# Attention and a mixture of experts in one kernel: a stack of its own for row-tiled scores, padded stacks for full-array distances, and a new order of down projection and scores

## What is computed

```python
B, S, D = 32, 256, 128            # x is (32, 256, 128); 16 heads of 8
x = x + attention(layernorm(x))   # attn = stablemax3(q k^T / sqrt(8)), out = attn v, then w_out and b_out
x = x + experts(layernorm(x))     # 4 experts of 512, the 2 best of each token by softmax of the router
# experts: h = silu(x w1[e]) * (x w3[e]); out = sum over e of gate[e] * (h w2[e])
# stablemax3(l): l -= max(l); s = 1/(1 - l(1 - l/2 (1 - l/3))) for l < 0; s / sum(s)
```

## Time and profile before

| | |
|---|---|
| three runs | 1270.7, 1271.81, 1272.38 us; median 1271.81 us |
| profiled execution | 1271.22 us, of which the span of the instructions is 1269.5 us |
| busy share | PE 89%, PEld 72%, DVE 78%, ACT 79%, POOL 57% |
| DMA | 77.58 MB, 19.7% of 16 DMA engines on the main queue |
| costliest groups | POOL L391 399.2 us; ACT L515 259.3 us; the three groups of PE L874 324.4, 293.4 and 292.9 us; DVE L651 308.5 us |
| mean granted TensorE clock | 0.980 |

### The profile page before, as it was taken

How to read it: one execution, slowest core, us unless ns; L and a number is a source line. 1 busy time by engine, 2 the same in 40 slices (tenths; PEclk the granted TensorE clock), 3 DMA queues, 4 the chain that set the end, 5 groups by cost and what they waited for, 6 DMA issues and landing times.

```text
span 1269.5 us, 29119 instructions
## 1 busy us (share of the span) xinstructions
PE 1135.1 (89%) x10116; PEld 911.3 (72%) x10116; DVE 985.9 (78%) x1804; ACT 1006.8 (79%) x1033; POOL 724.0 (57%) x961
## 2 busy tenths in 40 slices
PE   2569999899999999999999999999999999999987
PEld 1347777677877777777777787777777777778777
DVE  5678888788888887888888888888788887788632
ACT  1788888888888888888788888788888788888852
POOL 2426655565665556665556566555666555656554
PEclk9969999999999999999999999999999999999999
DMA  5112222102222211222211222221122221122000
GB/s 164 54 52 69 70 74 74 54 30 67 72 68 72 70 44 40 67 68 72 72 53 29 67 72 68 72 66 44 44 67 68 72 72 52 32 64 70 27 22 26
DMA packets 85034, 77.58 MB, mean 61 GB/s; under 512 B 11136, under 2 KB 79360, under 8 KB 84992
## 3 DMA queue, kind: packets, MB, share of 16 engines
q1 hardware_dynamic: 84560, 76.64, 19.7%
q10 hardware_dynamic: 432, 0.39, 0.1%
HBM read 53.81 MB, written 21.10 MB: 59 GB/s over the span
## 4 chain that ended last, share of the span: by engine, by line
PE 64%; DVE 15%; issue 12%; ACT 4%; DMA 2%; POOL 1%; DVEq 1%; SPq 0%; POOLq 0%; ACTq 0%
PE banks L874 21%; PE banks L1064 20%; PE sc L931 5%; PE banks L892 5%; DVE mx L727 4%; DVE hid L643 4%; PE sc L1049 3%; ACT w_sq L515 3%; DVE poly L651 2%; PE misc L1112 2%; PE misc L1015 2%; PE misc L1113 1%; PE misc L996 1%; POOL hid L391 1%; PE banks L1049 1%
## 5 line engine op out<-in xcount | busy, mean ns | idle before, releaser
L391 POOL TENSOR_TENSOR hid<-hid,gate_all 128x512 f32<-128x512 f32 x256 | 399.2, 1595 | 201.9 <-DMA gate_all<-gate_scratch 168.5
L515 ACT ACTIVATE w_sq<-sc 128x1024 f32<-128x1024 f32 x256 | 259.3, 1026 | 157.4 <-PE sc L931 157.1
L874 PE MATMUL banks<-xn_hi,w_hi 128*128 128x256 f32 x1024 | 324.4, 317 | 64.0 <-issue 28.5
L651 DVE SCALAR_TENSOR_TENSOR poly<-w_sq,sc 128x1024 f32<-128x1024 f32 x256 | 308.5, 1216 | 58.2 <-ACT w_sq L515 53.0
L874 PE MATMUL banks<-xn_lo,w_hi 128*128 128x256 f32 x1024 | 293.4, 287 | 0.0
L874 PE MATMUL banks<-xn_hi,w_lo 128*128 128x256 f32 x1024 | 292.9, 286 | 0.0
L874 PEld LDWEIGHTS banks<-xn_hi,w_hi 128*128 128x128 f32 x1024 | 197.6, 193 | 117.9 <-issue 75.9
L1064 PE MATMUL banks<-w_sb,hid 128*128 128x128 f32 x2048 | 268.0, 283 | 13.6 <-DVE hid L643 10.7
L1064 PEld LDWEIGHTS banks<-w_sb,hid 128*128 128x128 f32 x2048 | 240.0, 191 | 37.4 <-DVE hid L643 17.4
L727 DVE TENSOR_REDUCE mx<-sc 128x4 f32<-128x1024 f32 x192 | 228.5, 1220 | 42.2 <-PE sc L1049 40.4
L574 ACT ACTIVATE poly<-poly,two 128x2048 f32<-128x2048 f32 x128 | 254.9, 1992 | 0.4
(11 more groups left out here) (96 smaller groups left out, 1211.5 us busy)
## 6 DMA issues: line engine op xcount, KB each, us to landing
qk_scratch<-qk_split SPq DMA_DIRECT2D x32, 512.0 KB, 3.1
gate_all<-gate_scratch SPq DMA_DIRECT2D x32, 512.0 KB, 4.4
k_stack<-qk_scratch SPq DMA_DIRECT2D x96, 128.0 KB
q_stack<-qk_scratch SPq DMA_DIRECT2D x93, 128.0 KB
x_in<-in_L_attn_x_dram SPq DMA_DIRECT2D x32, 128.0 KB, 2.1
x_res<-in_L_attn_x_dram SPq DMA_DIRECT2D x32, 128.0 KB, 2.3
out_dram<-y_acc SPq DMA_DIRECT2D x32, 128.0 KB, 1.8
hid<-in_L_ffn_w_dram SPq DMA_DIRECT2D x2, 1024.0 KB, 6.5
```

The lines of the kernel that those rows point to most:

```text
L391: nc.gpsimd.tensor_tensor(h, h, by_token.unsqueeze(1).to_broadcast([128, 2, C, 128]), ALU.mult).then_inc(gated, 1)
L515: nc.scalar.activation(w_sq[:, u % 2, :], sc[:, u % 2, :], ACT.Square).then_inc(sq_ok, 1)
L651: nc.vector.scalar_tensor_tensor(poly[:, u, :], w_sq[:, u % 2, :], 3.0, sc[:, u % 2, :], ALU.add, ALU.mult).then_inc(poly_ok, 1)
L874: last = nc.tensor.matmul(dst, lhs[a], rhs[b], start=(k == 0), stop=(k == len(terms) - 1))
```

## The change

Scores and distances no longer share a stack.

- **Tiles for the scores.** q_tile and k_tile, one buffer each, hold the layout of 32 partitions a head, now with four terms (lo lo is added) and no row of maxima. Eight transfers fill them each step, of 128 KB. They wait until the scores of the sequence before are through (s_full).
- **Padded stacks for the distances.** q_stack has 8 groups of two heads, 64 partitions a head, row 8d + r; rows 124 to 127 take the maxima. k_pad holds for each head j of a pair its own 64 partitions and zeros elsewhere, which are written once at the start, as are the ones that meet the maxima. So a distance contracts over all 128 partitions and takes its head alone. Four transfers of 128 KB fill q_stack, eight of 64 KB fill k_pad. The matmuls' number and their 256 columns stay: 4 for a unit. Only units above 1 wait for poly_ok; unit 0 waits for the stacks and the maxima.
- **Order.** On TensorE score 0 stands ahead of the down projection, three of its units between score 0 and score 1, down(1,3) behind the transposes, maxima_T ahead of up_a of unit 0, and in the first half up_a of unit 6 ahead of the output projection. On VectorE maxima_out stands ahead of experts_added.
- **Wait.** up_a_unit(0) no longer waits for acc_ok.

```diff
-    STEP = 4
-    MROW, MSTEP = 3, 16
+    TERMS = 4
+    HALF = 64
+    MROW = 124
+    STEP = HALF // HD
+    GP = H // 2
...
-        q_stack = [sb(f"q_stack{i}", [128, G, S], F32R) for i in range(2)]
-        k_stack = [sb(f"k_stack{i}", [128, G, S], F32R) for i in range(2)]
-        no_maxima = sb("no_maxima", [8, S])
+        q_tile = sb("q_tile", [128, G, S], F32R)
+        k_tile = sb("k_tile", [128, G, S], F32R)
+        q_stack = [sb(f"q_stack{i}", [128, GP, S], F32R) for i in range(2)]
+        k_pad = [sb(f"k_pad{i}", [128, GP, 2, S], F32R) for i in range(2)]
+        ones = sb("ones", [2, S])
...
-        STACKED = 16 * 7
+        TILED = 16 * 2 * TERMS
+        STACKED = 16 * 12
...
-            eng.memset(k_stack[par][:].bitcast(F32), 1.0).then_inc(blank[par], 1)
+            eng.memset(k_pad[par][:].bitcast(F32), 0.0).then_inc(blank[par], 1)
...
+        def tile_rows(tile, r):
+            return tile[r::TERMS, :, :].bitcast(F32)
+
+        def tile_part(part):
+            return scratch[part].rearrange("(g e) t -> e g t", g=G)
...
         def stack_rows(stack, r):
             return stack[r::STEP, :, :].bitcast(F32)
 
         def stack_part(part):
-            return scratch[part].rearrange("(g e) t -> e g t", g=G)
+            return scratch[part].rearrange("(g e) t -> e g t", g=GP)
+
+        def pad_rows(pad, r, j):
+            return pad[HALF * j + r:HALF * (j + 1):STEP, :, j, :].bitcast(F32)
+
+        def pad_part(part, j):
+            return scratch[part].rearrange("(g j d) t -> j d g t", g=GP, j=2)[j]
...
+                    after(sp, tiled, tiles_read)
...
                 if has(i, off + 1):
+                    sp.wait_ge(qk_stored, stored_qk)
+                    after(sp, s_full, scored)
+                    for r, part in enumerate((1, 3, 1, 3)):
+                        sp.dma_start(tile_rows(k_tile, r), tile_part(part)).then_inc(tiled, 16)
+                    for r, part in enumerate((0, 0, 2, 2)):
+                        if isinstance(i, int) and n == -1:
+                            continue
+                        sp.dma_start(tile_rows(q_tile, r), tile_part(part)).then_inc(tiled, 16)
                     after(sp, w_full, w_used)
-                    sp.wait_ge(qk_stored, stored_qk)
                     if isinstance(i, int) and 0 <= n + 1 < 2:
                         sp.wait_ge(blank[par], 2)
-                    for r, part in enumerate((1, 3, 1)):
-                        sp.dma_start(stack_rows(k_stack[par], r), stack_part(part)).then_inc(stacked[par], 16)
-                    sp.dma_start(q_stack[par][MROW::MSTEP, :, :].bitcast(F32),
-                                 no_maxima[:].unsqueeze(1).to_broadcast([8, G, S])).then_inc(stacked[par], 16)
-                    for r, part in enumerate((0, 0, 2)):
+                        for j in range(2):
+                            sp.dma_start(k_pad[par][MROW + 2 * j:MROW + 2 * j + 2, :, j, :].bitcast(F32),
+                                         ones[:].unsqueeze(1).to_broadcast([2, GP, S])).then_inc(ones_in[par], 16)
+                    for r, part in enumerate((0, 0, 2, 2)):
                         if isinstance(i, int) and n == -1:
                             continue
                         sp.dma_start(stack_rows(q_stack[par], r), stack_part(part)).then_inc(stacked[par], 16)
+                    for r, part in enumerate((1, 3, 1, 3)):
+                        for j in range(2):
+                            sp.dma_start(pad_rows(k_pad[par], r, j), pad_part(part, j)).then_inc(stacked[par], 16)
...
-                    sp.dma_start(q_stack[par][MROW::MSTEP, :, :].bitcast(F32), m_split[:]).then_inc(m_stacked[par], 16)
+                    sp.dma_start(q_stack[par][MROW:, :, :].bitcast(F32), m_split[:]).then_inc(m_stacked[par], 16)
...
                 m = no(i, off)
                 after(pe, silu_ok, UP * m + u)
                 if u == 0:
-                    after(pe, acc_ok, m)
                     pe.wait_ge(xn2_lo_ok, m + 1)
                 up(u, up_a, w1_hi, w1_lo, a_full)
 
...
-            def distance_of(i, off, g, h, c):
-                par, rows = off % 2, slice(TILE * h, TILE * (h + 1))
-                at = (C * (h % 2) + c) * S
-                return nc.tensor.matmul(sc[:, h // 2, at:at + S], k_stack[par][rows, g, c * 128:(c + 1) * 128],
-                                        q_stack[par][rows, g, :], start=True, stop=True)
-
-            def first_distances(i, off):
+            def distances(i, off, u):
+
                 m, par = no(i, off), off % 2
-                pe.wait_ge(s_used, U * (m + 1))
-                pe.wait_ge(m_stacked[par], pair_count(i, off, 16))
-                for c in range(C):
-                    for h in range(4):
-                        op = distance_of(i, off, 0, h, c)
-                        if c == C - 1 and h % 2:
-                            op.then_inc(w_full, 1)
-
-            def distances(i, off, u):
-
-                m = no(i, off)
-                pe.wait_ge(poly_ok, U * m + u - 1)
-                for c in range(C):
-                    for h in (2 * (u % 2), 2 * (u % 2) + 1):
-                        last = distance_of(i, off, u // 2, h, c)
+                if u == 0:
+                    pe.wait_ge(s_used, U * (m + 1))
+                    pe.wait_ge(stacked[par], pair_count(i, off, STACKED))
+                    pe.wait_ge(m_stacked[par], pair_count(i, off, 16))
+                    if isinstance(i, int) and 0 <= m < 2:
+                        pe.wait_ge(ones_in[par], 32)
+                elif u > 1:
+                    pe.wait_ge(poly_ok, U * m + u - 1)
+                for j in range(2):
+                    for c in range(C):
+                        at = (C * j + c) * S
+                        last = nc.tensor.matmul(sc[:, u % 2, at:at + S], k_pad[par][:, u, j, c * 128:(c + 1) * 128],
+                                                q_stack[par][:, u, :], start=True, stop=True)
                 last.then_inc(w_full, 1)
...
-                if has(i, off):
-                    first_distances(i, off)
+                distance(0)
+                distance(1)
...
                 distance(6)
+                if has(i, off - 2):
+                    up_a_unit(i, off - 2, 6)
...
                     last.then_inc(res_full, 1)
-                if has(i, off - 2):
-                    up_a_unit(i, off - 2, 6)
                 distance(7)
...
                     if g == 0:
                         after(pe, poly_ok, U * m)
-                        pe.wait_ge(stacked[par], pair_count(i, off + 1, STACKED))
+                        pe.wait_ge(tiled, TILED * (m + 1))
...
-                                                  q_stack[par][rows, g, c * 128:(c + 1) * 128],
-                                                  k_stack[par][rows, g, :], start=True, stop=True)
+                                                  q_tile[rows, g, c * 128:(c + 1) * 128],
+                                                  k_tile[rows, g, :], start=True, stop=True)
...
                 down(0, 0)
                 down(0, 1)
-                score(0)
                 down(0, 2)
+                score(1)
                 down(0, 3)
```

More of the change, by code:

```diff
@@ L179, in attention_then_experts_kernel @@
         m_ok = sem("m_ok")
+        ones_in = [sem(f"ones_in{i}") for i in range(2)]
+        tiled = sem("tiled")
         m_stacked = [sem(f"m_stacked{i}") for i in range(2)]
@@ L527, in first_half @@
                     act.wait_ge(qk_stored, 16)
+                    for r, part in enumerate((0, 0, 2, 2)):
+                        nc.scalar.dma_start(tile_rows(q_tile, r), tile_part(part)).then_inc(tiled, 16)
                     act.wait_ge(blank[0], 2)
-                    for r, part in enumerate((0, 0, 2)):
+                    for r, part in enumerate((0, 0, 2, 2)):
                         nc.scalar.dma_start(stack_rows(q_stack[0], r), stack_part(part)).then_inc(stacked[0], 16)
@@ L840, in second_half @@
                     shifted_logits()
+                if has(i, off + 1):
+                    maxima_out()
                 if has(i, off - 2):
                     experts_added()
-                if has(i, off + 1):
-                    maxima_out()
                 if has(i, off + 2):
@@ L1114, in queries_and_keys @@
                                      stop=True).then_inc(qk_full, 1)
+                score(0)
                 down(0, 0)
                 down(0, 1)
-                score(0)
                 down(0, 2)
+                score(1)
                 down(0, 3)
-                score(1)
                 down(1, 0)
+                score(2)
                 down(1, 1)
-                score(2)
                 down(1, 2)
-                down(1, 3)
                 score(3)
@@ L1131, in second_half @@
                     queries_operand()
+                down(1, 3)
                 if isinstance(i, int) and n == 0:
@@ L1139, in second_half @@
```

(4 more changed lines are left out.)

21 lines of the change are left out of this document (11 added, 10 removed).

## The result

The changed kernel takes 1184.53 us (median of 4 runs, 1183.5 to 1186.13) against 1272.1 us, a ratio of 0.9314 (95% interval 0.9298 to 0.933). The forecast was 1199 us: right in sign and range, 14.5 us too slow.

The account below looks back on a forecast made before the run. No engine is full; TensorE's waits once per sequence, chiefly 1.60 us before the first up, were taken as the bound. 1271.2 - 67.3 (29 x (0.71 + 1.61)) - 8.3 clock + 3.5 start = 1199 us, range 1178 to 1228.

Parts of the forecast that it names:

- the clock: Lower-clock spells behind TensorE's long hole at up_a of unit 0 go with it: 8.3 us in 29 sequences.
- the start: First sequence: ten more transfers before the expert weights, 6.4 us, 2.95 hidden in ScalarE's idle: +3.5 us once.
- A: First half: distances on full arrays at 0.12 us each, first eight dearer, two small holes closed: -0.71 us a sequence.
- B: Behind the second weighted values: a wait of 0.58 us at up_b replaces one of 1.60: -1.61 us a sequence.
- C: Score 0 ahead of the down projection: work moved, not removed, 0 us; without it maxima_T would wait 0.7 us.
- D: ScalarE and POOL must follow the shorter sequence: ScalarE barely keeps up, POOL has no slack, no new wait.
- E: Stack transfers on SyncE's queue, seven to twenty a sequence, 0.64 us each in issue, all covered: 0 us.
- Rival 1: VectorE or POOL becomes the bound; maxima_T waits 0.7 us: 1220 us, up to 1228; chance 0.20.
- rival 4: An unseen 2.6 us wait a sequence, at up_b or maxima_T, takes all back: 1269 to 1274 us; chance 0.03.
- Rival 2: All holes close, the 0.58 us at up_b too; first eight distances cost at most 0.45: 1179 us; chance 0.13.
- Rival 3: Slower than before: scores wait for single-buffered tiles; at 1.6 us a transfer about 1311 us; chance 0.04.

Follow-up runs that it names:

- the order alone: Kernel before with the new order on TensorE and VectorE, up_a's wait for acc_ok kept, no stacks: 1200.7 us, ratio 0.9441.
- the stacks alone: Changed kernel with the old order and the old wait, so only tiles and padded stacks are new: 1280.95 us, ratio 1.0077.

## Why the prediction came out as it did

The sum was 2.32 us a sequence, 8.3 for the clock and 3.5 for the start. Measured: 2.89 a sequence, and 91.9 - 29 x 2.89 = 8.1 for what stood above the undisturbed period.

- **A, the padded distances: -0.71 forecast, -0.77 seen, but not theirs.** The price of 0.12 us for each held (a unit of twelve ups and four distances 1.91, forecast 1.92; the first eight 1.06, as 0.51 + 0.55 in the sum). The eight row-tiled ones went in at 0.51, their duration, though only 0.44 passes to the next start. Yet without the stacks, in the new order, the first half is 17.02 against 16.98. Compared group by group, the first eight cost 0.41 more, the next gaps save 0.71 in sum, the last group with its ups costs 0.26 more. The 0.48 for two small holes was two thirds of A, and the order closes both. They were also worth more than their idle: with the order alone, the stretch from the ups behind the second group of distances to the next transposes falls from 2.04 to 1.60, and that from the last distances to the last up from 2.90 to 2.56. That is 0.78, all of A. Where two edits can close one hole, I gave it to one.
- **B, wait and order behind the second weighted values: -1.61 forecast, -1.72 seen.** The idle left at up_b is 0.27 or less, not 0.58. I added whole durations of the copy and the add on VectorE; in the trace their starts are 0.34 apart though each takes 0.4. The six ups of up_a took 0.96 from their first start to the end of the last, not 0.72. The largest idle is where I put it.
- **C, score 0 ahead: 0 forecast, -0.40 seen. This step failed.** I wrote that work was moved, not removed, and that TensorE's path from the last up to the end of the second weighted values keeps its 13.5 us. It takes 13.15, because the down projection stood behind 0.35 us of idle for hid, and work moved in front of a wait covers it. The row was there and was not credited: 12 of the 14.5 us. The other half of C, that without it maxima_T would wait 0.7, was measured at 0.68.
- **D: nearly right.** ScalarE has no idle ahead of its L640 and 0.16 ahead of the first square; POOL costs TensorE 0.17 ahead of down(0,3), where I had none.
- **E: right for the tiles, blind for m_split.** The tiles have 4.1 us to spare; I had 3.6. But I followed the new transfers only. The old one got another destination and a landing of 3.0 us, in place of 2.06 in the last sequence and at most 2.4 in the steady ones. In the changed kernel it is hidden by 0.15 us (issue at 616.39, distances at 619.54) and sets the limit as soon as anything else improves.
- **The start: +3.5 forecast, +7.7 seen**, the term most wrong in ratio. The first m_split is issued 3.4 later, near the forecast; what I left out is that it then meets the expert weights and lands 5.26 behind its issue.
- **The clock: right in effect.** It fell in no steady sequence. But of the 8.3 us that I called the clock's, 1.1 was the sequence with the late m_split, at full clock; the lower clock explains some 7. Both are gone in the changed kernel, the second for no reason that I gave, so that part of the agreement is luck.

Seen less forecast, in us over the run: C -11.6, B -3.2, A -1.7, start +4.2, tail -0.9, clock and late transfer +0.2, together -13.0. The profiled execution took 1186.1, which is 13.0 below 1199.1; the median is another 1.6 below that.

Rival 1 did not occur and rival 4 neither. Rival 2's value (1179) was reached, but without the stacks and by another way. Rival 3 was real in its mechanism and far in margin.

## What to carry to other kernels

When work is moved ahead of a wait, credit it with the wait, and when two edits both sit next to a hole, price them in both orders, since only one can have it. When a layout changes, list every transfer whose destination changes, not only the new ones, and ask which partitions it writes. If removing an idle changes nothing, look for a second limit within some tenths of a microsecond: one run with both removed tells more than two with one each.

## What the runs showed of the hardware

- **Four neighbouring partitions take a transfer more slowly than four apart.** 32 rows of 1 KB, SBUF to SBUF, SP's queue, in the last sequence of each run, where all are measured alike: 2.99 to 3.03 us to partitions 124 to 127, 2.31 to 28, 60, 92 and 124, 2.06 to eight partitions 16 apart. In steady sequences it is 2.91 to 3.08 for the first and no more than 2.5 to 2.6 for the second. The issue took 0.70, 0.57 and 0.66 us. The Trainium skill (DMA: Bandwidth & Descriptors, Why a DMA increments its semaphore by 16 and not by 1) derives the number of engines from the slowest dimension, four in both of the first cases; by that alone nothing should have changed, and the measurement decides otherwise. The Trainium skill (DMA: Bandwidth & Descriptors, The descriptor swizzle) puts partitions 92 and 124 to 127 on one port and 28 and 60 on another. The runs fit that, but only two placements were tried, and the port as the cause is argued, not shown.
- **A short row-tiled group gains less than its tiles.** Eight distances over four tiles take 0.44 us to the next start, eight on full arrays 1.06, so 2.4 times as long. Four over two tiles cost with their switches 0.61, four on full arrays 0.48: there the tiles lose.
- **Where the clock fell.** The granted clock was 0.50, the 1.2 GHz level, behind holes of 1.60 to 1.66 us in eight sequences of before and eight of the stacks alone, and in every steady sequence behind holes of 2.81 to 3.96 with the tiles last. It stayed at full speed behind the other holes of 1.60 to 1.66, behind one of 1.46 (246.43) and behind all of 0.98 or less in the steady sequences.
